# Moving scan readouts and merge products of a two-stream kernel to GpSimd, and a softplus series to ScalarE

## What is computed

```python
x = layernorm(x + sparse_attention(x))   # 8 heads; 96 keys for each row: 64 local ones, 32 picked by top-k
x = layernorm(x + moe_top4(x))           # 16 experts in pairs, and a shared one
x = layernorm(x + state_space_scan(x))   # 256 channels, 16 states
x = layernorm(x + moe_top1(x))           # 8 experts with a capacity

# the rotated part of a query, wanted at two angles per row ("by place" and relative)
mu1, mu2 = split(softplus(q_r)); concat(mu1*cos - mu2*sin, mu1*sin + mu2*cos)
# the scan, for each state n of 16, over time t, all 256 channels
state = exp(delta*A[n]) * state + delta*u*B[n];   y += state * C[n]
# delta = softplus(...), computed as max(x, 0) + log1p(exp(-|x|))
# merge of the local and picked attention halves
out = (o_local*e0 + o_picked*e1) / (l_local*e0 + l_picked*e1)
```

## Time and profile before

| | us |
|---|---|
| median of 3 runs (lowest, highest) | 1208.69 (1207.24, 1210.38) |
| the profiled execution, its time | 1212.7 |
| the profiled execution, its span from first to last instruction | 1210.7 |
| VectorE (DVE) busy | 972.0 |
| TensorE (PE) busy | 844.6 |
| ScalarE (ACT) busy | 588.1 |
| GpSimd (POOL) busy | 194.3 |

### The profile page before, as it was taken

One profiled execution on the slowest core, in us unless ns is written; L12 is line 12 of the kernel. 1 busy time (PEld: TensorE's weight loads), 2 busy tenths in 40 slices (PEclk: granted clock), 3 DMA queues, 4 the chain that ended last, 5 costly groups with the idle time before them and its releaser, 6 DMA issues.

```text
span 1210.7 us, 29485 instructions
## 1 busy us (share of the span) xinstructions
PE 844.6 (70%) x11808; PEld 521.0 (43%) x11808; DVE 972.0 (80%) x2274; ACT 588.1 (49%) x1299; POOL 194.3 (16%) x104
## 2 busy tenths in 40 slices
PE   6666868877778774777676787485685577546774
PEld 3554656665545452443444555262253143212241
DVE  4757778876676868898989668888978699989978
ACT  4464636535436656524523586443574456533310
POOL 0000000000001100233200120034330065315500
PEclk9686978898968986698788898588997678768777
DMA  5102121101114012233101310424500353224200
GB/s 167 52 21 55 38 60 43 46 14 46 39 20 107 20 37 82 71 81 105 36 11 44 74 44 2 116 62 101 116 13 1 97 116 86 61 71 120 89 0 17
DMA packets 85080, 72.21 MB, mean 60 GB/s; under 512 B 24784, under 2 KB 63696, under 8 KB 84752
## 3 DMA queue, kind: packets, MB, share of 16 engines
q1 hardware_dynamic: 84944, 70.34, 22.6%
HBM read 66.51 MB, written 3.80 MB: 58 GB/s over the span
## 4 chain that ended last, share of the span: by engine, by line
DVE 44%; PE 26%; issue 14%; ACT 10%; DMA 3%; SPq 2%; POOL 1%; DVEq 0%; ACTq 0%; POOLq 0%
DVE bank L1887 10%; PE bank L819 5%; PE bank L632 4%; DVE Y L1975 4%; PE bank L854 3%; DVE XP L1891 2%; DVE CV L1891 2%; DVE ml L1620 2%; DVE onehot L1669 1%; SPq L566 1%; PE bank L978 1%; ACT relu_s L1150 1%; DVE CV L1839 1%; PE bank L918 1%; DMA RB<-rows_bounce 1%
## 5 line engine op out<-in xcount | busy, mean ns | idle before, releaser
L1446 POOL TENSOR_TENSOR big<-DU,BC 128x1024 f32<-128x1024 f32 x64 | 150.6, 2353 | 398.3 <-DVE DU L1874 204.9
L1887 DVE TENSOR_TENSOR_SCAN bank<-bank,big 128x512 f32<-128x512 f32 x128 | 156.8, 1225 | 4.7 <-ACT bank L1358 2.5
L1358 ACT ACTIVATE bank<-DEL,Aneg 128x512 f32<-128x512 f32 x128 | 87.5, 688 | 131.0 <-DVE XP L1891 57.5
L819 PE MATMUL bank<-onehot,tparts 128*32 128x256 bf16 x3840 | 125.4, 282 | 22.7 <-DVE onehot L1669 14.2
L819 PEld LDWEIGHTS bank<-onehot,tparts 128*32 128x32 bf16 x3840 | 100.3, 99 | 53.1 <-issue 28.2
L978 PE MATMUL bank<-XP,CO 128*128 128x512 f32 x128 | 75.6, 704 | 11.9 <-DVE XP L1891 11.9
L1669 DVE TENSOR_SCALAR onehot<-ib,CO 128x1024 bf16<-128x1024 f16 x160 | 76.6, 521 | 7.5 <-PE bank L819 6.8
L978 PE MATMUL bank<-CV,CO 128*128 128x512 f32 x128 | 69.0, 644 | 16.1 <-DVE CV L1891 16.0
L854 PE MATMUL bank<-GT,QBD 128*32 128x32 f32 x3072 | 59.1, 210 | 28.0 <-issue 18.3
L1150 ACT ACTIVATE relu_s<-bank,nml 128x192 f32<-128x192 f32 (+1 forms) x128 | 53.0, 426 | 40.6 <-DVE nml L1625 40.4
L854 PEld LDWEIGHTS bank<-GT,QBD 128*32 128x32 f32 x3072 | 56.3, 121 | 35.2 <-issue 34.9
(11 more groups left out here) (288 smaller groups left out, 1904.9 us busy)
## 6 DMA issues: line engine op xcount, KB each, us to landing
BC<-bc_rows SPq DMA_DIRECT2D x128, 256.0 KB, 4.4
ib<-idx_rows SPq DMA_DIRECT2D x64, 256.0 KB, 4.3
rows_bounce<-RO SPq DMA_DIRECT2D x256, 8.5 KB
big<-comb_rows SPq DMA_DIRECT2D x16, 256.0 KB, 5.1
big<-comb_rows SPq DMA_DIRECT2D x8, 512.0 KB, 8.8
W<-w SPq DMA_DIRECT2D x1, 2818.0 KB, 14.4
RB<-rows_bounce SPq DMA_DIRECT2D x16, 136.0 KB, 2.1
X<-x SPq DMA_DIRECT2D x4, 256.0 KB, 3.3
```

The source lines that it names most:

```text
L819: m = mm(own.bank[3 - c % 2][32 * bb:32 * bb + 32, 256 * kind:256 * kind + 256], own.tparts[:, kt, part, 32 * kind:32 * kind + 32], onehot ...
L1358: A(own.bank[STATE_BANKS[j]][:, :], own.DEL[:, j, :], ACT.Exp, scale=Aneg[:, j, n:n + 1]).then_inc(dA_ok.sem, dA_ok.up(b))
L1446: pool.tensor_tensor(own.dBu[:, n % 2, :, :], own.DU[:, :, :], own.BC[:, n % ROWS_AHEAD, 0:1, :].to_broadcast([P, 2, L]), ALU.mult).then_i ...
L1887: dve.tensor_tensor_scan(state, state, own.dBu[:, n % 2, j, :], 0.0, ALU.mult, ALU.add).then_inc(scan_ok.sem, scan_ok.up(b))
```

## The change

1. Readouts. Where `read_by_gpsimd(b, n)` holds (all n for b0 and b1, three of four for b2 and b3), the scan of the second half writes its states to SBUF (`hs`, two buffers), and GpSimd multiplies them by C[n]. VectorE no longer does the product. The exponential of the next state waits only for the scan in that half. In GpSimd's own order the readout of n-1 follows `dBu` of n.
2. Merge. VectorE stops after the reciprocal. GpSimd computes `fac`, the two products and the sum, from line 1532 on, for all 16 tiles.
3. Softplus. The polynomial of degree four is factored into two shifted squares. ScalarE squares r, then takes two `Square` activations with a bias. VectorE keeps the ratio, two combining operations, `DEL` and `DU`.
4. Turns. Both angles are done at once: two products on 128x512 and one subtraction and one addition on 128x256. The products go to `turns`, which lies in `relu_s`. The swapped copy on ScalarE now waits for both.
5. The order of the sections is laid anew on every engine. Counted off section by section, VectorE's new order lets the rests of b0 and b1 run ahead of the attention beside them (the scan of b1 is issued to its end before the last merge of b3; before, ten of its sixteen states were), and it interleaves the last two scans: the first state of b3 stands after state 6 of b2, so that ten states of each alternate. Before, the scan of b3 began after the scan of b2 had ended.

```diff
+def two_squares(c):
+
+    pairs = [r for r in np.roots(c[::-1]) if r.imag > 0]
+    return [(float(-r.real), float(r.imag) ** 2) for r in sorted(pairs, key=lambda r: r.real)]
+
+
+(SHIFT_1, REST_1), (SHIFT_2, REST_2) = two_squares(LOG1P)
+LEAD = LOG1P[4] ** 0.5
+
+
 class Signal:
 
...
-            own.muq, own.qr_c, own.qr_s = own.SR, own.SRd, own.PR
+            own.muq = own.SR
+            own.turns = own.relu_s[:, :, :].rearrange("p a c -> p (a c)")[:, 0:1024].rearrange("p (s c) -> p s c", s=2)
             own.krot = own.PR[:, :, :].rearrange("p (s n) c -> p s n c", s=2)
             own.QAB = sb("QAB", [P, 2, NH, 2, 32])
...
             return b >= 2 and i < 2
+
+        def read_by_gpsimd(b, n):
+
+            return b < 2 or n % 4 != 3
+
+        def readout(b, n, j):
+
+            if j == 0:
+                return read_1.sem, read_1.at(b, n + 1)
+            by = read_g if read_by_gpsimd(b, n) else read_2
+            return by.sem, by.at(b, sum(read_by_gpsimd(b, k) == read_by_gpsimd(b, n) for k in range(n + 1)))
 
         def query_spread(b, i):
 
...
                 A(own.dt_c, own.dt_c, ACT.Exp, scale=-1.0).then_inc(dt_sp.sem, dt_sp.up(b))
+                yield PART
+                act.wait_ge(sr_ok.sem, sr_ok.at(b, 1))
+                A(own.dt_c, own.dt_a, ACT.Square).then_inc(act_s.sem, act_s.up(b))
+                act.wait_ge(act_s.sem, act_s.now(b))
+                A(own.dt_b, own.dt_c, ACT.Square, bias=shift[:, 0:1]).then_inc(sq_ok.sem, sq_ok.up(b))
+                act.wait_ge(sq_ok.sem, sq_ok.now(b))
+                A(own.dt_c, own.dt_c, ACT.Square, bias=shift[:, 1:2], scale=LEAD).then_inc(sq_ok.sem, sq_ok.up(b))
                 yield
...
+                            if j == 1 and read_by_gpsimd(b, n - 1):
+                                act.wait_ge(scan_ok.sem, scan_ok.at(b, 2 * n))
+                            else:
+                                act.wait_ge(*readout(b, n - 1, j))
                         A(own.bank[STATE_BANKS[j]][:, :], own.DEL[:, j, :], ACT.Exp, scale=Aneg[:, j, n:n + 1]).then_inc(dA_ok.sem, dA_ok.up(b))
                     if n >= 1:
...
         def gpsimd_program(pool):
+            PT = pool.tensor_tensor
+
+            def merge(b, i):
+
+                own = attentions[b]
+                yield PART
+                pool.wait_ge(den_ok.sem, den_ok.at(b, i + 1))
+                pool.wait_ge(em_ok.sem, em_ok.at(b, i + 1))
+                pool.wait_ge(own.rb_in.sem, own.rb_in.at(b, i + 1))
+                PT(own.fac[:, :, :], own.em[:, :, :], own.den[:, 3, :].unsqueeze(1).to_broadcast([P, 2, NH]), ALU.mult).then_inc(pool_s.sem, pool_s.up(b))
+                pool.wait_ge(pool_s.sem, pool_s.now(b))
+                PT(own.On[:, 1, :, :], own.RB[:, :, 0:DC], own.fac[:, 1, :].unsqueeze(2).to_broadcast([P, NH, DC]), ALU.mult).then_inc(pool_s.sem, pool_s.up(b))
+                pool.wait_ge(ol_sb.sem, ol_sb.at(b, i + 1))
+                PT(own.On[:, 0, :, :], own.On[:, 0, :, :],
+                   own.fac[:, 0, :].unsqueeze(2).to_broadcast([P, NH, DC]), ALU.mult).then_inc(pool_s.sem, pool_s.up(b))
+                pool.wait_ge(pool_s.sem, pool_s.now(b))
+                PT(own.On[:, 0, :, :], own.On[:, 0, :, :], own.On[:, 1, :, :], ALU.add).then_inc(on_ok.sem, on_ok.up(b))
+                pool.wait_ge(on_ok.sem, on_ok.now(b))
+
             def keys(b):
                 for _ in range(KEY_PHASES):
                     yield
...
+                    if i >= 1:
+                        yield from merge(b, i - 1)
+                    for _ in range(TILE_PHASES - 2):
+                        yield
 
             def merges(b):
-                for _ in range(MERGE_PHASES):
+                yield
+                yield
+                yield from merge(b, NT - 1)
+                for _ in range(MERGE_PHASES - 2):
                     yield
...
-                    if n >= 1:
-                        pool.wait_ge(scan_ok.sem, scan_ok.at(b, 2 * (n - 1) + 1))
-                    row_in = own.row_in[n % ROWS_AHEAD]
-                    pool.wait_ge(row_in.sem, row_in.at(b, 2 * (n // ROWS_AHEAD) + 2))
-                    pool.tensor_tensor(own.dBu[:, n % 2, :, :], own.DU[:, :, :], own.BC[:, n % ROWS_AHEAD, 0:1, :].to_broadcast([P, 2, L]),
-                                       ALU.mult).then_inc(dBu_ok.sem, dBu_ok.up(b))
-                    yield
+                for n in range(DS + 1):
+                    if n < DS:
+                        if n >= 1:
+                            pool.wait_ge(scan_ok.sem, scan_ok.at(b, 2 * (n - 1) + 1))
+                        row_in = own.row_in[n % ROWS_AHEAD]
+                        pool.wait_ge(row_in.sem, row_in.at(b, 2 * (n // ROWS_AHEAD) + 2))
+                        pool.tensor_tensor(own.dBu[:, n % 2, :, :], own.DU[:, :, :], own.BC[:, n % ROWS_AHEAD, 0:1, :].to_broadcast([P, 2, L]),
+                                           ALU.mult).then_inc(dBu_ok.sem, dBu_ok.up(b))
+                    if n >= 1 and read_by_gpsimd(b, n - 1):
+                        yield PART
+                        pool.wait_ge(scan_ok.sem, scan_ok.at(b, 2 * n))
+                        if n >= 3:
+                            pool.wait_ge(ysum.sem, ysum.at(b, 2 * (n - 3) + 2))
+                        pool.tensor_tensor(own.hC[(n - 1) % 2][:, 1, :], own.hs[:, (n - 1) % 2, :], own.BC[:, (n - 1) % ROWS_AHEAD, 1, :],
+                                           ALU.mult).then_inc(read_g.sem, read_g.up(b))
...
                 dve.wait_ge(em_ok.sem, em_ok.at(b, i + 1))
-                dve.wait_ge(ol_sb.sem, ol_sb.at(b, i + 1))
                 TT(own.den[:, 0, :], own.ll[:, :], own.em[:, 0, :], ALU.mult)
                 TT(own.den[:, 1, :], own.RB[:, :, 33], own.em[:, 1, :], ALU.mult).then_inc(vec.sem, vec.up(b))
                 dve.wait_ge(vec.sem, vec.now(b))
                 TT(own.den[:, 2, :], own.den[:, 0, :], own.den[:, 1, :], ALU.add).then_inc(vec.sem, vec.up(b))
                 dve.wait_ge(vec.sem, vec.now(b))
-                dve.reciprocal(own.den[:, 3, :], own.den[:, 2, :]).then_inc(vec.sem, vec.up(b))
-                dve.wait_ge(vec.sem, vec.now(b))
-                TT(own.fac[:, :, :], own.em[:, :, :], own.den[:, 3, :].unsqueeze(1).to_broadcast([P, 2, NH]), ALU.mult).then_inc(vec.sem, vec.up(b))
-                dve.wait_ge(vec.sem, vec.now(b))
-                TT(own.On[:, 0, :, :], own.On[:, 0, :, :],
-                   own.fac[:, 0, :].unsqueeze(2).to_broadcast([P, NH, DC]), ALU.mult)
-                TT(own.On[:, 1, :, :], own.RB[:, :, 0:DC], own.fac[:, 1, :].unsqueeze(2).to_broadcast([P, NH, DC]), ALU.mult).then_inc(vec.sem, vec.up(b))
-                dve.wait_ge(vec.sem, vec.now(b))
-                TT(own.On[:, 0, :, :], own.On[:, 0, :, :], own.On[:, 1, :, :], ALU.add).then_inc(on_ok.sem, on_ok.up(b))
-                dve.wait_ge(on_ok.sem, on_ok.now(b))
+                dve.reciprocal(own.den[:, 3, :], own.den[:, 2, :]).then_inc(den_ok.sem, den_ok.up(b))
+                dve.wait_ge(den_ok.sem, den_ok.now(b))
 
             def merge_c(b, i):
...
-
-                    for s, tmp in ((cos, tc), (sin, tsn)):
-                        m = TT(tmp.rearrange("p n (k c) -> p n k c", k=2), src.rearrange("p n (k c) -> p n k c", k=2),
-                               s.unsqueeze(1).unsqueeze(1).to_broadcast([P, n, 2, HALF]), ALU.mult)
+                def rotate(i):
+
+                    both_turns = own.turns.rearrange("p s (k g c) -> p s k g c", k=2, c=HALF)
+                    src = own.muq[:, :, :].rearrange("p h (k c) -> p (h k) c", k=2).unsqueeze(1).to_broadcast([P, 2, 2 * NH, HALF])
+                    for s in range(2):
+                        m = TT(both_turns[:, s, :, :, :], src, trig[:, s, i:i + 5:4, :].unsqueeze(2).to_broadcast([P, 2, 2 * NH, HALF]), ALU.mult)
                     m.then_inc(vec.sem, vec.up(b))
                     dve.wait_ge(vec.sem, vec.now(b))
-                    TT(dst[:, :, 0:HALF], tc[:, :, 0:HALF], tsn[:, :, HALF:DR], ALU.subtract)
-                    TT(dst[:, :, HALF:DR], tc[:, :, HALF:DR], tsn[:, :, 0:HALF], ALU.add).then_inc(done.sem, done.up(b))
-                    dve.wait_ge(done.sem, done.now(b))
+                    tc, tsn = (own.turns[:, s, :].rearrange("p (k h c) -> p k h c", k=2, c=DR) for s in range(2))
+                    TT(own.QAB[:, :, :, 1, 0:HALF], tc[:, :, :, 0:HALF], tsn[:, :, :, HALF:DR], ALU.subtract)
+                    TT(own.QAB[:, :, :, 1, HALF:DR], tc[:, :, :, HALF:DR], tsn[:, :, :, 0:HALF], ALU.add).then_inc(q_rows.sem, q_rows.up(b))
+                    dve.wait_ge(q_rows.sem, q_rows.now(b))
 
                 def index_sum(t):
                     Wt = index_width(t)
...
-                TT(own.dt_a, own.dt_b, own.dt_c, ALU.mult).then_inc(vec.sem, vec.up(b))
-                dve.wait_ge(vec.sem, vec.now(b))
-                TT(own.dt_c, own.dt_a, own.dt_a, ALU.mult).then_inc(vec.sem, vec.up(b))
-                dve.wait_ge(vec.sem, vec.now(b))
```

(35 more changed lines are left out.)

41 lines of the change are left out of this document (24 added, 17 removed), and 65 rows, old and new, of the table ORDER.

## The result

The changed kernel takes 1170.01 us in the median of four runs (1168.04 to 1172.66), against 1209.54 us for the kernel before in the same job. The ratio is 0.9667, with a 95% interval of 0.9625 to 0.971: 40 us, or 3.3%, faster. The forecast was 1160 us in a range of 1124 to 1198. The profiled execution took 1168.04 us, with a span of 1166.3 us and a mean granted TensorE clock of 0.841 of full speed; in the kernel before it was 0.819.

A forecast was written before the change was run, and what follows sets the result against it. VectorE, 80% busy, was taken as the bound wherever a scan runs. Of 90 us taken off it, stages let through 51.5, less 3 for late merges, 48.5: 1212.7 to 1164 profiled, 1160 us median, range 1124 to 1198.

The forecast's parts named there:

- the four terms: VectorE work taken off: readouts 38.8 us, softplus 17.5, turns 10.5, merge 23.2.
- The sum of 90 us: Whole kernel: VectorE loses 90 us of 972 through readouts, softplus, turns and merge.
- the line through two prices: GpSimd's merge: prices at 1024 and 512 elements give 0.77 us at 256, 0.27 at 16.
- the product of 2.33 us: Earlier trace: a VectorE two-SBUF product needing 0.69 us took 2.33 beside a GpSimd product, said to end with it.
- `dBu` 3.7 us apart where a scan is alone: Scan running alone: `dBu` starts about 3.7 us apart, from 3.86; readout move gains 0.14 us a state.
- One-hots above 0.75 us in the scans: Sign in b0's and b1's scans: VectorE's one-hots, sharing ports with GpSimd, rise above 0.75 us.
- only a quarter: Attention, 0 to 350 us: a quarter of 16.8 us saved on VectorE comes through, 4 us.
- most of the rest: b0's scan: 15.3 us saved, less 3 for dearer one-hots, mostly comes through, 10 us.
- second rival: GpSimd becomes the scans' clock at 3.65 us a state plus handovers; gain 20 us, 1189 us; chance 0.19.
- The end: Last stage: 24 readouts and a softplus, 21 us, less `dBu` loop and blocked products, give 14 us.
- the first (all the freed time used, 1125): Whole kernel: freed VectorE time is used nearly whole, 1209 - 84 = 1125 us; chance 0.18.
- The third (1233): Slower: VectorE operations and GpSimd wait for each other over the shared ports, 72 us more, 1233 us; chance 0.08.

The follow-up runs named there:

- order_only: The changed kernel with all four parts undone, so the new order alone (and without VectorE's end-of-state wait): 1214.72 us, ratio 1.0051 to the kernel before.
- head_back: The changed kernel with the 32 readouts of b0 and b1 back on VectorE, the 24 of b2 and b3 staying on GpSimd: 1171.38 us, ratio 0.9679.

## Why the prediction was right, and where not

The direction and the size hold: 1170 us lies in the forecast's own range of 1142 to 1180. The mechanism, VectorE time set free that comes through in part, holds for the whole, but not where the sum put most of it. The mechanisms that made up the sum were these, with what was found.

- VectorE's busy time: 885 forecast, 890.1 found. The order took 15 us off (956.9 in order_only), which no term had, and the parts took 67 and not 90. Form by form, from order_only to after, the four terms are as they were sized: readouts 38.7 us, merge 23.3, softplus 17.4, turns 10.0. What stayed on VectorE became dearer by 17 us (durations times counts), led by the one-hots with 5.4. The other 6 us are that durations overlap in the records (a readout of 0.69 us starts at 1042.17 and the next scan at 1042.78), so that 0.69 counts as 0.61. The sum of 90 us, made of durations, was too high by that. The order's gift and the dearer work nearly cancel.
- GpSimd: 308 forecast, 299.4 found. Readouts cost 1.29 us as forecast. Merge products cost 0.62 to 0.73 and not 0.77, so the lower bound (half of a 512-wide one) was nearer than the line through two prices.
- The scan to SBUF costs nothing more (1.209), as taken. The squares on ScalarE cost 1.056 and, with a bias, 1.148; no switch of function shows. VectorE waits 6.0 us for them, in three of the four batches, 2.0 each.
- The earlier trace rows was read slightly wrong: the product of 2.33 us did not end when GpSimd did (990.38 + 2.35 = 992.73) but 0.54 us later (990.94 + 2.33 = 993.27), so that it ran after the wait. Nothing in the sum hangs on it.
- `dBu` 3.7 us apart where a scan is alone: 3.70. But the step from 3.86 is not the readout's. order_only has 3.72 with all readouts on VectorE, because VectorE's wait at the end of a state is gone, so moving the readout brings 0.02 us a state and not 0.14. The 3.83 us of VectorE work that the text put into a state are durations that overlap; the four instructions take 3.72. Pairs 6.9 us apart: 6.6. One-hots above 0.75 us in the scans: 0.744 and 0.794. 72 readouts on VectorE. VectorE's share towards 77%: 76%.
- Turns: 10.5 us, of which attention was to let through a quarter. The step that failed is that only a quarter gets through there. The stretch ahead of b0's scan gave 20.6 us in the two traces, 16 with the mean of the seven kernels that share it (470.4), and 14 to 17 at like clocks, where the sum had 8. Undone one at a time, the merge costs 8 to 11 us there and the turns 5 to 8. VectorE isn't full in attention, but its turns and its merge lie on the path; through which waits is open, since TensorE's wait for the turned query is longer after (48.4 us) than before (28.6).
- Readouts in the scans of b0 and b1: the sum had 10 us in each stage. The step that failed is "most of the rest": the traces have 1.2 and 2.8 us, and head_back shows that the 32 readouts there bring nothing. The text held the reason ready, as its second rival: a loop of 3.65 to 3.72 us a state. Its argument against that rival, that b0's scan took 7.6 us a state because attention lies between, was wrong where it matters. The states that run alone take 3.70 us with the readout on GpSimd and 3.72 without, and in the others the dearer one-hots and merge steps take their share. The sign that it named for the second rival, a GpSimd without a gap in b0's scan, did not come even so: GpSimd was busy for 60.7 of 95.2 us there.
- The end: 14 us forecast, 19.4 found (6.5 + 12.2 + 0.7), most of it in the pairs. The tail's 24 readouts were the better part of the 56.
- The order: no term in the sum. Alone it costs 0.5%, 6 us. So the parts gave 46 us (forecast 48.5) and the order took 6 back: that is most of the 10 us between 1160 and 1170. That the sum of the parts came out right is in good part luck, since the stages, by the two traces, were off by +13 ahead of b0's scan (+6 to +9 at like clocks), by -22 from there to the end of b1's, and by +7 in the last three.

Of the rivals, the first (all the freed time used, 1125) needed VectorE's share to stay at 80%; it fell to 76%. The second (1189) was right about b0 and b1, wrong about the tail and the merges. The third (1233) asked for means above 1.5 us in products of two SBUF tiles. The expert products average 0.69, as the order had moved them away from the scans; in the old order, with the parts, they do rise, to 1.17 and 1.06. That is still below 1.5, and that kernel was faster than the one before, so the third rival fails in either order; the new order took away most of what it had. The Trainium skill's rule of the exclusive lock ("SBUF — State Buffer", section "SBUF: two separate sides") agrees with this: whichever starts first has the pair, and the other blocks. The product of 5.90 us, against 1.22 alone, shows that GpSimd can come first again, twice, while VectorE waits.

## What to carry to other kernels

Before work goes from a full engine to a half-empty one, look at what hands the two their work in turn: where a loop of both (here scan, `dBu`, scan, 3.70 us) is as long as the work that stays, the freed time becomes a wait, and only a second stream laid beside it makes it pay. Short chains in a stage that no engine fills can pay more than a busy share suggests. The list of waits did not tell which ones; undoing the parts one at a time and comparing marks did, at a like granted clock. And an order that gains nothing alone can be what makes a change pay, so the two should be measured together and apart.

## What the runs showed of the hardware

- A VectorE product of two SBUF tiles was held up by GpSimd instructions that start after it: 5.90 us instead of 1.22, behind one readout and two `dBu` that ran without a gap. Room for GpSimd to run ahead is a risk for VectorE, then.
- The wait hits the fast one-input forms too: one-hots of 0.48 us average 0.74 and 0.79 beside a GpSimd that is 53% to 59% busy. The scan with one PSUM and one SBUF input isn't touched (1.21 to 1.23 us on the mean in every trace), nor does it matter to it whether it writes to PSUM or to SBUF.
- Two-input products cost GpSimd 2.36 us for 1024 elements, 1.29 for 512, 0.62 to 0.73 for 256 and 0.32 for 16: about 1.9 times VectorE's time at 512 (0.69).
- The same instructions in the same order took between 465.9 and 475.7 us up to b0's scan in seven profiled executions, at mean granted clocks of 0.88 to 0.84, while the pieces in which VectorE is full repeat closely (`DU` of b3 to its last scan: 92.0 or 92.1 in all six kernels that have the same work there). For a small effect in one stage the piece tells more than the whole, and where TensorE is busy the clock belongs beside it.
